# Row projections in two halves: one PSUM bank each, filled and evacuated apart, in a two-attention layer kernel

## The reference

```python
# attention over the batch-local sequence, 16 heads of 16, without a mask
x_proj = (x @ w_in.T + b_in).reshape(b, l, h, -1)
q, k, v = jnp.split(x_proj, 3, axis=-1)
att = softmax(einsum('blhd,bmhd->blmh', q, k) * scale, axis=2)
opt = einsum('blmh,blhd->blhd', att, v)      # every row of att sums over m, v keeps its own row
x = layernorm(x + opt.reshape(b, l, d) @ w_out.T + b_out)
# routed attention: mean router logits of a batch pick 4 of 16 heads of 64
dist = softmax(mean(x @ Wr + br, axis=1)); idx = sort(top_k(dist, 4))
Qs, Ks, Vs = gather of (x @ W + bias) for the picked heads
O = softmax(Qs @ Ks.T / 8) @ Vs
x = layernorm(x + O @ Wo + bo)
```

## Time and profile before

| what | value |
|---|---|
| median of 3 runs | 3857.26 us (3854.34 to 3864.57) |
| the profiled execution | 3870.09 us |
| its span | 3868.3 us |
| mean granted clock of PE | 0.948 |
| busy: PE, DVE, ACT, POOL | 3528.3, 3338.0, 3064.0, 1807.8 us |

### The profile page before, as it was taken

How to read it: one execution, slowest core, us unless ns; L and a number is a source line. 1 busy time by engine, 2 the same in 40 slices (tenths; PEclk the granted TensorE clock), 3 DMA queues, 4 the chain that set the end, 5 groups by cost and what they waited for, 6 DMA issues and landing times.

```text
span 3868.3 us, 42407 instructions
## 1 busy us (share of the span) xinstructions
PE 3528.3 (91%) x14172; PEld 1276.6 (33%) x14172; DVE 3338.0 (86%) x3292; ACT 3064.0 (79%) x5065; POOL 1807.8 (47%) x1319
## 2 busy tenths in 40 slices
PE   8889889789999999899999999899999999899997
PEld 3323323332232323343232323343232323343333
DVE  7999999989999999778999999878999999267776
ACT  6999999769999998788989998788999998333333
POOL 4334333304444346344434346344444346758665
PEclk9988888889999999899999999899999999899998
DMA  5222221200010001200000001200000000100000
GB/s 159 87 79 79 79 85 61 84 15 17 17 28 17 22 22 42 69 13 24 17 22 22 22 22 42 69 14 23 17 23 22 22 22 19 46 1 12 11 12 11
DMA packets 117195, 142.65 MB, mean 37 GB/s; under 512 B 33394, under 2 KB 100466, under 8 KB 116978
## 3 DMA queue, kind: packets, MB, share of 16 engines
q1 hardware_dynamic: 116978, 139.95, 12.3%
HBM read 89.55 MB, written 50.33 MB: 36 GB/s over the span
## 4 chain that ended last, share of the span: by engine, by line
PE 45%; DVE 29%; ACT 16%; issue 5%; POOL 3%; SPq 1%; DMA 1%; DVEq 0%; POOLq 0%; ACTq 0%
DVE nmax L1292 20%; ACT ps L1107 13%; PE ps L1063 10%; PE ps L963 9%; PE ps L1028 7%; PE ps L1043 7%; DVE smax L1352 6%; PE ps L938 5%; PE ps L923 4%; PE ps L1078 1%; POOL y L770 1%; PE ps L1046 1%; DVE st L1271 1%; POOL facc L874 1%; PE ps L932 1%
## 5 line engine op out<-in xcount | busy, mean ns | idle before, releaser
L1292 DVE TENSOR_REDUCE nmax<-ps 128x1 f32<-128x1024 f32 x2048 | 2381.8, 1217 | 212.9 <-PE ps L963 206.4
L1107 ACT ACTIVATE ps<-ps,nmax 128x1024 f32<-128x1024 f32 x2048 | 2233.7, 1100 | 284.6 <-DVE nmax L1292 258.0
L963 PE MATMUL ps<-stack 96*128 96x512 bf16 x4500 | 1332.6, 402 | 202.4 <-ACT ps L1107 123.4
L874 POOL TENSOR_TENSOR facc<-facc,probs 128x1024 f32<-128x1024 f32 x443 | 1041.9, 2352 | 751.6 <-ACT probs L1221 660.9
L963 PEld LDWEIGHTS ps<-stack 96*128 96x128 bf16 x4500 | 325.5, 100 | 1322.2 <-ACT ps L1107 822.2
L1352 DVE TENSOR_REDUCE smax<-ps 128x2 f32<-128x1024 f32 x512 | 619.4, 1218 | 138.9 <-PE ps L1028 138.3
L1028 PE MATMUL ps<-fk,fq 64*128 64x512 f32 x2048 | 572.1, 641 | 34.6 <-ACT ps L1107 30.6
L1043 PE MATMUL ps<-fq,fk 64*128 64x512 f32 x2048 | 553.6, 619 | 26.3 <-DVE smax L1352 16.0
L1063 PE MATMUL ps<-probs,vals 128*64 128x512 f32 x2048 | 516.1, 611 | 1.8
L1221 ACT ACTIVATE probs<-ps 128x1024 f32<-128x1024 f32 x384 | 391.8, 1020 | 74.5 <-PE ps L1046 74.1
L1107 ACT ACTIVATION_READ_ACCUMULATOR ps<-ps,nmax 128x1 f32 x2048 | 433.1, 211 | 0.0
(11 more groups left out here) (129 smaller groups left out, 2020.9 us busy)
## 6 DMA issues: line engine op xcount, KB each, us to landing
stack<-qk_levels SPq DMA_DIRECT2D x768, 64.0 KB, 2.2
qk_levels<-fk SPq DMA_DIRECT2D x64, 384.0 KB, 2.5
probs<-in_L_attn_x SPq DMA_DIRECT2D x16, 512.0 KB, 4.1
v_rows<-vals SPq DMA_DIRECT2D x16, 512.0 KB, 3.7
vrows<-v_rows SPq DMA_DIRECT2D x16, 512.0 KB, 3.4
res<-in_L_attn_x SPq DMA_DIRECT2D x16, 512.0 KB, 4.2
x_rows<-y SPq DMA_DIRECT2D x16, 512.0 KB, 2.9
res<-x_rows SPq DMA_DIRECT2D x16, 512.0 KB, 3.9
```

Source lines behind the costliest of these rows:

```text
L874: pool.tensor_tensor(total, total, probs[:, slot, :], ALU.add).then_inc(facc_ready, 1)
L963: last = pe.matmul(bank(banks[i]), stack[0:SK, hd % 2, 0, t * P:(t + 1) * P], stack[0:SK, hd % 2, 1, col:col + CH], start=True, stop=True)
L1107: act.activation(src, src, ACT.Exp, bias=nmax[:, b % 2, half, t, hd:hd + 1], scale=-1.0, accum_out=esum[:, b % 2, half, t, hd:hd + 1]).the ...
L1292: dve.tensor_reduce(nmax[:, b % 2, half, t, hd:hd + 1], two_banks(banks), AX.XY, ALU.min).then_inc(min_ready, 1)
```

## The change

Each of VP, FV, OP and FO becomes two halves of two row tiles. A half takes one bank when its first part starts (parts 0 and 2), and each half has a reader of its own: VPh and VP, FVh and FV on ACT, OPh and OP, FOh and FO on DVE. `filled` rises after part 1 and after part 3, and there are new semaphores `v_half`, `vals_half` and `y_half`. `add_rows` is called twice: each call adds 512 columns and takes two bn_stats; the second also takes the four bn_aggr. The residual, the slot of `y` and X1 of its former user are waited for by the first call. POOL's bias adds stay whole and wait for both halves. In the plan a half copy on ACT costs 0.6 us (the whole 1.0), the halves of `add_rows` 1.45 and 1.75 (the whole 3.1).

```diff
+HALVES = ("VP", "FV", "OP", "FO")
-URGENT = ("J", "AT", "OT", "OP", "X1", "RT")
+URGENT = ("J", "AT", "OT", "OP", "OPh", "X1", "RT")
...
-            banks_of[name] = banks if i == 0 else 0
-            if i == 0:
-                reader[name] = read_by
+            banks_of[name] = 0
+            if tag[0] in HALVES and i % 2 == 0:
+                banks_of[name] = 1
+                reader[name] = read_by if i else read_by[:1] + (tag[0] + "h",) + tag[1:]
+            elif i == 0:
+                banks_of[name], reader[name] = banks, read_by
...
-        unit(act("VP", b, c), 1.0, [pe("VP", b, c)] + ([sp("SV", "VP", *jobs[i - 2][1:])] if i >= 2 else []))
+        unit(act("VPh", b, c), 0.6, [pe("part", 1, "VP", b, c)] + ([sp("SV", "VP", *jobs[i - 2][1:])] if i >= 2 else []))
+        unit(act("VP", b, c), 0.6, [pe("VP", b, c), act("VPh", b, c)])
...
-            unit(act("FV", b, c), 1.0, [pe("FV", b, c)])
+            unit(act("FVh", b, c), 0.6, [pe("part", 1, "FV", b, c)])
+            unit(act("FV", b, c), 0.6, [pe("FV", b, c), act("FVh", b, c)])
...
-        unit(dve(*t), 3.1, [pe(*t), pool("RB", *t)] + free)
+        unit(dve(k + "h", b, c), 1.45, [pe("part", 1, *t), pool("RB", *t)] + free + ([dve(*norms[i - 1])] if i else []))
+        unit(dve(*t), 1.75, [pe(*t), dve(k + "h", b, c)])
...
-                if t == TPC - 1:
+                if (t + 1) % 2 == 0:
                     last.then_inc(filled, 1)
...
-                elif kind == "VP":
-                    i = job_no[at]
+                elif kind in ("VPh", "VP"):
+                    i, half = job_no[at], kind == "VP"
                     if i >= 2:
                         act.wait_ge(v_out[i % 2], i // 2 * 16)
-                    rows = v_new[:, i % 2, :, :].rearrange("p (a t) d -> p a (t d)", a=2)
-                    act.activation(rows, two_banks(banks), ACT.Copy).then_inc(v_copied, 1)
+                    rows = v_new[:, i % 2, 2 * half:2 * half + 2, :].rearrange("p t d -> p (t d)")
+                    act.activation(rows, bank(banks[half]), ACT.Copy).then_inc(v_copied if half else v_half, 1)
...
-            def add_rows(t, banks):
+            def add_rows(t, half, into):
                 i = norm_no[t]
-                s = i % 2
-                dve.wait_ge(res_ready, i + 1)
+                s, two = i % 2, slice(2 * half, 2 * half + 2)
+                if not half:
+                    dve.wait_ge(res_ready, i + 1)
...
-                rows = lambda buf: buf[:, s, :, :].rearrange("p (a t) d -> p a (t d)", a=2)
-                dve.tensor_tensor(rows(y), two_banks(banks), rows(res), ALU.add).then_inc(y_ready, 1)
-                dve.wait_ge(y_ready, i + 1)
-                for r in range(TPC):
+                added = y_ready if half else y_half
+                rows = lambda buf: buf[:, s, two, :].rearrange("p t d -> p (t d)")
+                dve.tensor_tensor(rows(y), bank(into), rows(res), ALU.add).then_inc(added, 1)
+                dve.wait_ge(added, i + 1)
+                for r in (2 * half, 2 * half + 1):
                     last = dve.bn_stats(st[:, s, r, :], y[:, s, r, :])
                 last.then_inc(bn_ready, 1)
-                dve.wait_ge(bn_ready, i * BN_STEPS + 1)
-                for r in range(TPC):
-                    last = dve.bn_aggr(mv[:, s, r, :], st[:, s, r, :])
-                last.then_inc(bn_ready, 1)
+                if half:
+                    dve.wait_ge(bn_ready, i * BN_STEPS + 2)
+                    for r in range(TPC):
+                        last = dve.bn_aggr(mv[:, s, r, :], st[:, s, r, :])
+                    last.then_inc(bn_ready, 1)
```

More of the change, by code:

```diff
@@ L408, in plan @@
                 if banks_of[n]:
-                    held[n] = pick(banks_of[n])
-                    held[n[:1] + n[3:] if n[1] == "part" else n] = held[n]
+                    held[n] = tuple(pick(banks_of[n]))
+                    whole = n[:1] + n[3:] if n[1] == "part" else n
+                    if whole != n:
+                        held[whole] = held.get(whole, ()) + held[n]
                     free.difference_update(held[n])
@@ L582, in build, with filling @@
         order, held, freed, again, planned = plan()
-        fill_no = {n[1:]: i + 1 for i, n in enumerate(n for n in order["PE"] if n in held and n[1] not in ("V", "part"))}
+        def filling(n):
+            if n[1] == "part":
+                return (n[3] + "h",) + n[4:] if n[3] in HALVES and n[2] == 1 else None
+            return n[1:] if n in held and n[1] != "V" else None
+        fill_no = {t: i + 1 for i, t in enumerate(t for t in map(filling, order["PE"]) if t)}
         nth = {}
@@ L950, in _ @@
                         pe.wait_ge(rt, was[2] * ROUTE_STEPS + 2)
+                    elif was[1] in ("OPh", "FOh"):
+                        pe.wait_ge(y_half, norm_no[(was[1][:2],) + was[2:]] + 1)
                     elif was[1] in ("OP", "FO"):
@@ L1096, in _ @@
                 tile = n[1:]
-                banks = held.get(("PE",) + tile)
+                banks = held.get(("PE", kind[:2]) + at)
                 if banks and kind not in ("A", "RT", "V"):
@@ L1168, in _ @@
                                    bias=bqk_sel[:, 0, p:p + 1]).then_inc(fq_ready, 1)
-                elif kind == "FV":
+                elif kind in ("FVh", "FV"):
                     b, c = at
+                    half = kind == "FV"
                     if b:
@@ L1177, in _ @@
                             act.wait_ge(v_out[s], len(jobs) // 2 * 16)
[L1178 to L1181 removed]
+                    rows = vals[:, c * TPC + 2 * half:c * TPC + 2 * half + 2, :].rearrange("p t d -> p (t d)")
+                    act.activation(rows, bank(banks[half]), ACT.Copy).then_inc(vals_copied if half else vals_half, 1)
+                elif kind in ("VPh", "VP"):
+                    i, half = job_no[at], kind == "VP"
                     if i >= 2:
                         act.wait_ge(v_out[i % 2], i // 2 * 16)
[L1184 to L1185 removed]
+                    rows = v_new[:, i % 2, 2 * half:2 * half + 2, :].rearrange("p t d -> p (t d)")
+                    act.activation(rows, bank(banks[half]), ACT.Copy).then_inc(v_copied if half else v_half, 1)
                 elif kind == "LN":
@@ L1283, in _ @@
                 kind, at = n[1], n[2:]
-                banks = held.get(("PE",) + (("T",) + at if kind == "C" else n[1:]))
+                banks = held.get(("PE", "T" if kind == "C" else kind[:2]) + at)
                 if banks and kind != "M":
@@ L1314, in _ @@
                         dve.reciprocal(both[:, 0, :], whole).then_inc(total_ready, 1)
+                elif kind in ("OPh", "FOh"):
+                    add_rows((kind[:2],) + at, 0, banks[0])
                 elif kind in ("OP", "FO"):
-                    add_rows(n[1:], banks)
+                    add_rows(n[1:], 1, banks[1])
                 elif kind == "NM":
```

22 lines of the change are left out of this document (12 added, 10 removed).

## The result

The kernel after takes 3800.74 us (median of 4 runs, 3793.97 to 3805.75), the kernel before beside it 3858.91 us (4 runs). The ratio is 0.9843, 95% interval 0.9829 to 0.9856: 58 us or 1.6% faster. The prediction was 3849 (3825 to 3880), so the result lies under its range. The profiled execution has a span of 3803.9 us.

The account below looks back on a forecast made before the run. PE, DVE and ACT near 92% were taken to bound two stages together, PE alone the last. Terms +5.5 - 1.3 - 3.8 - 4.2 - 4.5 = -8.3 us took 3857.3 to 3849 us, range 3825 to 3880.

Parts of the forecast that it names:

- In the last stage only PE counts: Last batch's second attention: PE is at 97% while DVE and ACT have room; no gain was costed for its FO.
- SP's queue gets nothing new: Transfers wait for the second half as they waited for the whole, so the transfer queue adds no cost.
- The closing sentence on one greedy run: The forecast is wrong if the new plan shuffles tiles far from the projections; a moved unit moves all behind it.
- The price: Extra evacuation instructions: ACT's split copies +1.7 us and DVE's split add_rows +3.8 us, together +5.5 us.
- rival 2: DVE or ACT queues wait for a half PE hasn't finished; at 0.5 us each +17 us, 3874; chance 0.20.
- The end: After the run's last matmul only the second half of add_rows is left, 1.84 us instead of 3.11: gain 1.27 us.
- VP: First stage: the first half copy fills ACT's hole, so the next tile comes earlier; 14 x 0.3 us, 4.2 us gained.
- Seams: Last OP of four seams: earlier first half brings the second attention's weights sooner; 3.8 us gained of 5.1 at most.
- FO between seams: Nine FO: the first half of add_rows fills DVE's hole; 0.5 us each, 4.5 us gained.
- the step costed at nothing: Banks: halves still break pairs, and PE does not stand still where a pair is freed, so no gain was counted.
- Rival 3: Banks were the shortage: PE's idle time around VP and DVE's between seams vanish; 24 us gained, 3833; chance 0.18.

Follow-up runs that it names:

- order only: The kernel before with the order planned for halves with banks held together, each row projection still evacuated whole: 3838.26 us, ratio 0.9936.
- all together: All four row projections evacuated in halves, each taking and giving back its two banks together, against the kernel before: 3822.90 us, ratio 0.9900.
- VP alone: The kernel before with only VP filled and evacuated in halves, planned anew: 3857.41 us, ratio 0.9996.

## Why the prediction was wrong, point by point

A gain was forecast and a gain came, but that is luck as far as the forecast's reasons go: the halves in the old order lose 11 us. By ratios the 1.57% splits along these kernels into 0.64 (order only), 0.36 (halves at work in that order), 0.40 (FO's own banks) and 0.17 (the others' banks, which can't be told from nothing), or about 25, 14, 15 and 7 us. The table puts the 14 into the last stretch alone (443.5 to 429.1).

- **The step that failed first** is the one that left the last batch out: "In the last stage only PE counts", and three of its FO had no term in the sum. The rows bore out that PE is the bound there, at 97%. But the missing 3% held PE's waits behind VectorE, 6.33, 6.04 and 4.17 us, and each brought the lower clock with it. The change took 21 us of this away, once halves and the new order came together. I had averaged over 400 us, and looked at 8 us windows only in the other two stages.
- **The second** is that the change was costed in before's order. Planned anew, the order alone gives 25 us. "SP's queue gets nothing new" held for its entries and not for their sequence, which is worth 20 us in after and 7 in before. The closing sentence on one greedy run named this as what would make the forecast wrong, but gave it neither size nor width. The two replannings show the size: 13 and 19 us for a change of 0.1 us in one price.
- **The price** (+5.5 us): the DVE pair came out exact (2 x 0.682 - 1.212 = 0.15 us). The ACT pair by durations is 2 x 0.61 - 1.015 = 0.21 us in place of 0.16. In before's order the halves with all their gains cost 11 us net, so rival 2 was nearer than the forecast for that kernel. Its sign doesn't show, though: the idle time that grew is that for a store, not for PE.
- **The end** (-1.3 us): right. The chain of waits at the end of after has the last matmul until 3789.54 + 6.23 = 3795.77 and then:

```profile
3795.80 0.70 DVE y L1289
3796.50 0.02 issue
3796.52 0.77 DVE st L1292 x2
3797.29 0.02 issue
3797.31 0.39 DVE mv L1297 x4
```

  That is 1.93 us in place of 3.11; 1.84 was foreseen.
- **VP** (-4.2 us): the size came, the picture not quite. In the 8 us window PE idles 0.67 us in place of 0.83, and ACT is busy for 8.00 in place of 7.51. But VP stands elsewhere in the new order: POOL is busy for 7.55 us in that window, where it was 1.65 on average, and the half copy at 256.79 stands between two exponentials with no hole before it. The first stage is 4.1 us shorter by the medians of three traces each; what of this is the filled hole and what the new place isn't separated. VP alone gives 0.9996, 1.5 us, which can't be told from nothing.
- **Seams** (-3.8 us): the mechanism named, the last OP's earlier first half, was not what counted. Against the medians of before (831.5, 870.5, 870.0) order only gains 4, 7 and 6.5 us in the three cycles (827.0, 863.5, 863.5), and all together, with the halves at work, adds nothing to it (826.1, 863.4, 863.5). Of the rest of the 30 us that after gains in the second and third, 11 go with FO's own banks.
- **FO between seams** (-4.5 us): the half as a filler of DVE's hole is worth nothing that the table shows, since order only and all together agree in those rows to 1 us. What gave something was the step costed at nothing, FO's halves in separate banks.
- **Rival 3** (banks, 3833) had the nearest time, yet its mechanism, PE idle for lack of pairs around VP, is not what happened: own banks for VP, FV and OP give some 7 us, which can't be told from nothing. Whether FO's banks win through room or through the order that the planner then finds stays open, since every change of banks replans.

## What to carry over

When a change goes through a greedy planner, its own mechanism and the new order are two changes. Run the new order with the old instructions, the old order with the new ones, and one meaningless replanning, before anything is said of the mechanism. In a stage whose bound is at 97%, look at what the missing 3% are: here it was three waits of 4 to 6 us, and slower matmuls after each. Small operations of VectorE in front of a queue that feeds PE are best kept clear in time of POOL's long adds; here that took both an earlier start and a place ahead of the tiles. And two traces are not enough for steps of 10 us: the same order took 841.5 us in one execution and 831.5 in another.

## What the runs showed of the hardware

A VectorE operation of 0.16 us on 128x4 elements took 2.27 us, fourteen times as long, when it started inside a 2.34 us add of POOL, and `y` operations of 0.41 us took 2.4. It is not all of VectorE's work. These maxima and subtractions, which read PSUM, ran in after beside POOL's adds (3562.41 to 3567.27 and from 3567.42) at their usual length:

```profile
3564.69 1.22 DVE L1406 TENSOR_TENSOR probs<-ps,stack 128x1024 f32<-128x1024 f32 x1 [1.70 <-PE ps L1061]
3567.62 2.36 DVE L1376 TENSOR_REDUCE smax<-ps 128x2 f32<-128x1024 f32 x2 [1.70 <-PE ps L1046]
```

The Trainium skill (SBUF — State Buffer, SBUF: two separate sides) says that VectorE and GpSimd share one pair of SBUF ports, which whoever starts first locks for its whole instruction, against a VectorE operation with two SBUF inputs (if the GpSimd operation reads SBUF) or in a 2-port mode. The trace agrees: the operations held up take all their inputs from SBUF, and the two above have at most one input there. In which mode an operation ran, no trace here shows.

PE's granted clock fell from 1.00 to 0.50 within the waits of 6.33 and 6.04 us in the last batch of before and 1 us behind the one of 4.17 us. Before the first of them it had been 1.00 through 178 us without a gap in PE's work. Each time it was back at 1.00 about 7 us later.
